# Two heads' scores in 64 array rows each, unpadded keys, one copy for q and k, one score buffer of two banks, scores behind the products of a step

## The reference

```
n = layer_norm(x);  x = x + attention(n, n)            # self:  20 heads of 64, 128 queries, 128 keys
n = layer_norm(x);  x = x + attention(n, context)      # cross: 20 heads of 64, 128 queries, 77 keys
x = geglu_ff(layer_norm(x)) + x
# layer 1: 20 heads of width 8, 73 text keys and 4 image keys, softmax, mask, output product, residual
attention: sim = (q @ k.T) * 64**-0.5; p = softmax(sim); out = p @ v; out @ wo + bo
```

## Time and profile before

| what | value |
|---|---|
| median of 3 runs | 3806.16 us (3804.15 to 3810.74) |
| span of the profiled execution | 3799.1 us |
| TensorE matmul busy | 3608.9 us, 95% |
| TensorE weight loads busy | 3328.8 us, 88% |
| VectorE, ScalarE, GpSimd busy | 2547.7, 2592.4, 1352.4 us |
| mean granted TensorE clock | 0.995 |

### The profile page before, as it was taken

The page is one execution under the profiler, slowest core; times in us unless marked ns, Lnnn a source line. Parts: engine busy times, 40 slices in busy tenths (PEclk is TensorE's granted clock), DMA queues, the critical chain, the costliest instruction groups (busy, mean ns, idle before and its releaser), DMA issues.

```text
span 3799.1 us, 88944 instructions
## 1 busy us (share of the span) xinstructions
PE 3608.9 (95%) x29708; PEld 3328.8 (88%) x29708; DVE 2547.7 (67%) x8159; ACT 2592.4 (68%) x8021; POOL 1352.4 (36%) x1658
## 2 busy tenths in 40 slices
PE   6999999999999999999999999999999999999997
PEld 5888989889898898988989899898988989889897
DVE  6667666676766666676676766767667676666766
ACT  6667676766767667676676766767676676766764
POOL 2233343333433334333333433334333343333433
PEclk9999999999999999999999999999999999999998
DMA  6522314223142321413223132231422313232130
GB/s 169 163 64 75 103 44 119 60 85 91 41 122 58 96 77 51 123 47 106 70 60 117 45 112 65 76 103 44 121 57 87 90 41 121 58 96 77 53 93 18
DMA packets 210716, 313.38 MB, mean 82 GB/s; under 512 B 31232, under 2 KB 167520, under 8 KB 210272
## 3 DMA queue, kind: packets, MB, share of 16 engines
q1 hardware_dynamic: 209984, 307.53, 27.6%
q10 hardware_dynamic: 288, 0.16, 0.0%
HBM read 267.97 MB, written 14.42 MB: 74 GB/s over the span
## 4 chain that ended last, share of the span: by engine, by line
PE 60%; DVE 17%; ACT 11%; issue 8%; POOL 4%; DMA 1%; SPq 0%; ACTq 0%; DVEq 0%; POOLq 0%
PE PS L818 8%; PE PT L840 6%; PE PV L854 6%; PE PW L798 5%; PE PG L659 5%; ACT SE L989 4%; PE PG L651 4%; PE PG L634 4%; PE PV L864 3%; DVE sums L1233 3%; PE PG L637 3%; PE PG L635 3%; PE PG L636 3%; POOL SE L1404 3%; PE PG L742 2%
## 5 line engine op out<-in xcount | busy, mean ns | idle before, releaser
L1404 POOL TENSOR_TENSOR SE<-SE,rs 128x512 f32<-128x512 f32 (+1 forms) x640 | 557.6, 871 | 1761.8 <-DVE rs L1238 1761.8
L989 ACT ACTIVATE SE<-PS,mx 128x128 f32<-128x128 f32 (+2 forms) x3840 | 982.6, 346 | 240.7 <-DVE qq L1262 128.5
L975 ACT ACTIVATE PTs<-PT 128x512 f32<-128x512 f32 (+2 forms) x960 | 575.4, 599 | 87.1 <-PE PT L840 67.9
L840 PE MATMUL PT<-ident,SE 128*128 128x128 f32 (+2 forms) x3840 | 582.0, 274 | 36.4 <-POOL SE L1404 34.6
L1233 DVE TENSOR_REDUCE sums<-SE 128x4 f32<-128x512 f32 (+1 forms) x640 | 367.0, 573 | 337.8 <-ACT SE L989 336.9
L1222 DVE TENSOR_REDUCE mx<-PS 128x4 f32<-128x512 f32 (+2 forms) x960 | 504.4, 525 | 72.1 <-PE PS L818 58.7
L840 PEld LDWEIGHTS PT<-ident,SE 128*128 128x128 f32 (+2 forms) x3840 | 465.5, 144 | 64.5 <-POOL SE L1404 49.0
L1396 POOL TENSOR_TENSOR n<-qq,p_half 128x4 f32<-128x4 f32 x320 | 345.3, 1079 | 490.2 <-DVE qq L1262 490.1
L798 PE MATMUL PW<-w_o,OTs 128*128 128x160 f32 x2560 | 415.3, 299 | 1.1 <-ACT OTs L967 1.1
L818 PE MATMUL PS<-qk 128*128 128x256 f32 x1280 | 348.5, 395 | 47.6 <-ACT qk L915 47.6
L912 ACT ACTIVATE qk<-PG 128x256 f32<-128x256 f32 x640 | 252.9, 395 | 190.1 <-PE PG L637 186.5
(11 more groups left out here) (207 smaller groups left out, 7828.5 us busy)
## 6 DMA issues: line engine op xcount, KB each, us to landing
q_slice<-q_split SPq DMA_DIRECT2D x630, 192.0 KB, 2.4
vc_slice<-vc_split SPq DMA_DIRECT2D x155, 512.0 KB, 3.6
kc_slice<-kc_split SPq DMA_DIRECT2D x150, 256.0 KB, 2.7
q1st<-q_hi SPq DMA_DIRECT2D x320, 32.0 KB, 1.9
k1st<-k_hi SPq DMA_DIRECT2D x160, 38.5 KB, 1.9
xres<-in_x_dram SPq DMA_DIRECT2D x32, 160.0 KB, 2.3
q1st<-q_lo SPq DMA_DIRECT2D x160, 32.0 KB, 1.9
out_dram<-x SPq DMA_DIRECT2D x64, 80.0 KB, 1.6
```

Of the source, the lines that this page charges most:

```text
L840: last = tr(PT[0:J, 128 * i:128 * i + 128], SE[:, place % 4, J * i:J * i + J], ident[:, :])
L975: a_(PTs[0:J, place % 3, :], PT[0:J, :], ACT.Copy).then_inc(S["pts_done"], 1)
L989: last = a_(SE[:, place % 4, J * i:J * i + J], PS[place % 2][:, step * i:step * i + J], ACT.Exp, bias=mx[:, place % 2, i:i + 1])
L1404: gp.tensor_tensor(e, e, rs[:, n % 2, :].unsqueeze(2).to_broadcast([128, 4, J]), ALU.mult)\
```

## The change

- q is scaled by SCALE0 when its weights are split (SPLIT_SCALE, `slice_high`, `slice_low`), not when it is copied out.
- Job "qk" is read out by one copy of 512 (self) or 256 columns (cross) in place of three or one; "kc" by one copy on each of ScalarE and VectorE in place of two. Keys are no longer padded, and the memsets for the padding go.
- The scores of a head take 64 rows of the array: four matmuls of 128 or 77 columns for a unit, alternately on rows 0 to 63 (into bank 0 of PS) and rows 64 to 127 (into bank 1).
- PS is one buffer of two banks: `scores` waits for the exponentials of the unit just before.
- On TensorE `scores` moves from the start of a step behind `probs_v`; `probs_transposed` moves behind "v" and `wo`. The lists of the other engines keep their order.

```diff
-        PS = [ctx.enter_context(nc.psum_tensor(f"PS{i}", [128, 512], fp32)) for i in range(2)]
+        PS = ctx.enter_context(nc.psum_tensor("PS", [128, 2, 512], fp32))
...
                 def scores(u):
                     place, (layer, g, n) = PLACE[u], u
-                    if place >= 2:
-                        pe.wait_ge(S["exp_done"], place - 1)
-                        layer0, g0, n0 = UNITS[place - 2]
-                        if layer0 == "l1":
-                            pe.wait_ge(S["sip_in"], l1_count(g0, n0))
-                    ps = PS[place % 2]
+                    if place >= 1:
+                        pe.wait_ge(S["exp_done"], place)
...
-                        keys = qk[:, n % 2, 1:3, :]
+                        keys = qk[:, n % 2, 1, :]
...
                         for b in range(HB):
-                            last = mm(ps[:, 2 * J * b:2 * J * b + 2 * J], qk[:, n % 2, 0, 128 * b:128 * b + 128],
-                                      keys[:, :, J * b:J * b + J], start=True, stop=True)
+                            for e in range(2):
+                                rows = slice(DH * e, DH * e + DH)
+                                last = mm(PS[:, e, J * b:J * b + J],
+                                          qk[rows, n % 2, 0, 128 * b:128 * b + 128],
+                                          keys[rows, J * b:J * b + J], start=True, stop=True)
...
                 for t in range(FIRST, LAST):
                     if t == KEEP_BUSY:
                         keep_busy(20)
-                    if t + 1 in UNIT_AT:
-                        scores(UNIT_AT[t + 1])
                     for name in qk_at(t):
                         job(name)
-                    if t - PT_LAG in UNIT_AT:
-                        probs_transposed(UNIT_AT[t - PT_LAG])
                     for name in late_at(t):
                         if name[0] == "v":
                             job(name)
                     for u in outputs_at(t):
                         if u[0] == "l0":
                             wo(*u[1:])
+                    if t - PT_LAG in UNIT_AT:
+                        probs_transposed(UNIT_AT[t - PT_LAG])
                     for u in products_at(t):
                         probs_v(u)
+                    if t + 1 in UNIT_AT:
+                        scores(UNIT_AT[t + 1])
...
                     elif kind == "qk":
                         ps = take(name)
-                        last = a_(qk[:, i % 2, 0, :], ps[:, 0:HT], ACT.Copy, scale=SCALE0)
-                        if i < U0:
-                            for e in range(2):
-                                last = a_(qk[DH * e:DH * e + DH, i % 2, 1 + e, :], ps[DH * e:DH * e + DH, HT:2 * HT],
-                                          ACT.Copy)
-                        last.then_inc(S["qk_done"], 1)
+                        w = 2 if i < U0 else 1
+                        a_(qk[:, i % 2, 0:w, :].rearrange("p a n -> p (a n)"), ps[:, 0:w * HT], ACT.Copy)\
+                            .then_inc(S["qk_done"], 1)
```

More of the change, by code:

```diff
@@ L267, in _ @@
                 nc.vector.memset(gv[:, :, :, :], 1.0)
-                nc.vector.memset(qk[:, :, :, :], 0.0)
             @block.gpsimd
@@ L984, in exp @@
                             act.wait_ge(S["qq_done"], l1_count(g0, n0))
-                    J, step = (K0[n // U0],) * 2 if layer == "l0" else (TT, T)
+                    J = K0[n // U0] if layer == "l0" else TT
                     if layer == "l1":
@@ L988, in exp @@
                     for i in range(4):
-                        last = a_(SE[:, place % 4, J * i:J * i + J], PS[place % 2][:, step * i:step * i + J], ACT.Exp,
-                                  bias=mx[:, place % 2, i:i + 1])
+                        scored = PS[:, i // 2, J * (i % 2):J * (i % 2) + J] if layer == "l0" else PS[:, 0, T * i:T * i + J]
+                        last = a_(SE[:, place % 4, J * i:J * i + J], scored, ACT.Exp, bias=mx[:, place % 2, i:i + 1])
                     last.then_inc(S["exp_done"], 1)
@@ L1148, in job @@
                         if (g, i) == (0, 0):
-                            dve.wait_ge(keys_zero, 1)
+                            dve.wait_ge(S["split_done"], 6)
                         dve.wait_ge(S["kc_done"], NP * g + i + 1)
-                        for e in range(2):
-                            rows = slice(DH * e, DH * e + DH)
-                            last = v.tensor_copy(kx[1][rows, i, e, :].rearrange("p (b t) -> p b t", t=T),
-                                                 ps[rows, HB * TS:2 * HB * TS].rearrange("p (b t) -> p b t", t=TS)[:, :, 0:T])
-                        last.then_inc(S["kc_dve"], 1)
+                        v.tensor_copy(kx[1][:, i, 0, :].rearrange("p (b t) -> p b t", t=T),
+                                      ps[:, HB * TS:2 * HB * TS].rearrange("p (b t) -> p b t", t=TS)[:, :, 0:T])\
+                            .then_inc(S["kc_dve"], 1)
                     elif kind == "v":
@@ L1219, in softmax_in @@
                     dve.wait_ge(S["s_done"], place + 1)
-                    J, step = (K0[n // U0],) * 2 if layer == "l0" else (TT, T)
-                    sc = PS[place % 2][:, 0:4 * step].rearrange("p (i j) -> p i j", j=step)
-                    v.tensor_reduce(mx[:, place % 2, :], sc[:, :, 0:J], AX, ALU.max, negate=True).then_inc(S["mx_done"], 1)
-                    if layer == "l1":
+                    if layer == "l0":
+                        J = K0[n // U0]
+                        sc = PS[:, :, 0:2 * J].rearrange("p e (b j) -> p e b j", j=J)
+                        v.tensor_reduce(mx[:, place % 2, :].rearrange("p (e b) -> p e b", b=2), sc, AX, ALU.max, negate=True)\
+                            .then_inc(S["mx_done"], 1)
+                    else:
+                        sc = PS[:, 0, 0:4 * T].rearrange("p (i j) -> p i j", j=T)
+                        v.tensor_reduce(mx[:, place % 2, :], sc[:, :, 0:TT], AX, ALU.max, negate=True).then_inc(S["mx_done"], 1)
                         b, w = n // W1, n % W1
@@ L1292, in split_low @@
                             rows = slice(M * r, M * r + M)
-                            last = v.tensor_tensor(hi[rows], raw[rows], hi[rows].bitcast(fp32), ALU.subtract)
+                            last = v.scalar_tensor_tensor(hi[rows], raw[rows], scale, hi[rows].bitcast(fp32),
+                                                          ALU.mult, ALU.subtract)
                         last.then_inc(S["split_done"], 1)
```

42 lines of the change are left out of this document (20 added, 22 removed).

## The result

| | before | after |
|---|---|---|
| median | 3808.45 us (4 runs, 3804.15 to 3812.24) | 4536.1 us (4 runs, 4529.21 to 4540.7) |
| ratio | | 1.191, 95% interval 1.1895 to 1.1928 |
| profiled span | 3799.1 us | 4538.9 us |
| TensorE busy | 3608.9 us, 95% | 3907.6 us, 86% |
| TensorE idle (span less busy) | 190 us | 631 us |

The change made the kernel 19% slower, 436 us more than the 4100 us forecast, and beyond the upper end of the range (4420). Of the 740 us of span, 441 are TensorE's idle time (269 in the forecast) and 299 its busy time (28 in the forecast).

A forecast was written before the change was run, and what follows sets the result against it. TensorE, 95% busy, was the bound. 3799.1 + 28 - 48 + 267 + 17 + 23 + 70 - 60 = 4096 us of span, plus 7 to the median, said as 4100; forecast 4020 to 4180, range 3900 to 4420.

The forecast's parts named there:

- The pauses for banks that VectorE frees: TensorE jobs wait for bank reads queued behind the late scores' maxima: 20 jobs a group, 16.7 us a group, +267 us.
- The 17 us for ScalarE's copy of q: Three jobs a group wait for ScalarE's copy of q, which stands behind the exponentials: 0.35 us each, +17 us.
- the 60 us taken as covered: Part of the new TensorE waits falls on pauses that exist already: -60 us, between 0 and 142.
- The single chain behind `unit_out`: TensorE stands still from the scores' end through maxima, `unit_out` and the "kc" read: 2.2 us a pause.
- faster with free banks: Rival: VectorE's bank reads end before TensorE asks, no new wait comes, 3786 us; chance 0.06.
- 0.44 + 0.09 + 0.09 = 0.62: Split score group on TensorE: 0.44 us for four pairs of matmuls, 0.09 for each drain entering and leaving the tile size.
- Tiles in turn: Rival: the split score matmuls run one behind the other, a pair costs 0.22 us, 4380 us in all; chance 0.18.
- The halved scores: Rival: changing tile size costs nothing, no pause comes, each score group's busy time halves, 3467 us; chance 0.03.
- +28 us of occupancy: Score matmuls split by rows on TensorE: self units -39 us, cross units +67 us, together +28 us.
- the loop of the single buffer: Scores wait for exponentials to free the one buffer: 1.93 us between self groups, four short steps a group, +23 us.
- the later probabilities, +70 us: Probabilities reach PT 4.0 us after the scores end; nine places a group are short, 0.48 us each, +70 us.
- the 48 that went: TensorE's wait for ScalarE's copy of q and k ahead of the scores, 47.6 us, goes: -48 us.

The follow-up runs named there:

- e7_reads_first: The changed kernel with VectorE reading the kc and v banks ahead of the maxima of the next unit: 4298 us, ratio 1.129.
- e2_pos_one: The kernel before with the scores in the late place, also waiting for the exponentials of the unit just before, as with one buffer: 4618 us, ratio 1.213.
- e5_rows: The changed kernel with the qk and kc copies of the kernel before, scores still split by rows: 4572 us, ratio 1.201.
- e6_filled: The changed kernel with unused identity matmuls behind the scores of four units in groups 1 to 14: 4463 us, ratio 1.172.
- e3_se5: The changed kernel with five SE buffers for the exponentials' results in place of four: 4412 us, ratio 1.160.
- e1_pos: The kernel before with only TensorE's order changed: scores behind `probs_v`, PT behind v and `wo`, both score buffers kept: 4504 us, ratio 1.183.
- e4_a_first: The changed kernel with TensorE's order of before, scores at the start of the step, one score buffer kept: 5505 us, ratio 1.447.

## Why the prediction was wrong, and where it was right

In one paragraph: the chain that the forecast built on was right in kind and size, and the sum over it was too short by 436 us. It counted a pause as its idle time and nothing else, with the clock left where it was, and it left out three waits (for an SE buffer, for a table load, and of `wo`). The place of the scores was put at 246 us and cost 699.

**Right: the direction, and the term it rested on.** The pauses for banks that VectorE frees were put at 267 us. The rows rose from 77 to 335, by 258. That is so near that some luck is in it, since not every wait came as long as counted (three of the five pauses of about 2 us). The 17 us for ScalarE's copy of q did not come (4.4 us). Nor is there a sign of the 60 us taken as covered: rows that stood before stand unchanged, such as PT's 34.6 and 34.1 us. The single chain behind `unit_out` was 2.13 us for 2.2, and e7_reads_first removed it as the mechanism demands. The rival "faster with free banks" is out: its limit was 20 us of new pauses.

**Right: how split tiles run.** A self group of the changed kernel (L776 is another job's transposition):

```profile
1184.04 0.71 PE L813 MATMUL PS<-qk 64*128 64x128 f32 x8
1184.69 0.33 PE L776 MATMUL PG<-ident,o 128*128 128x128 f32 x1
```

From L813's first start to the next instruction it takes 0.65 us, and 0.60 for cross (1538.14 to 1538.74, where L631 started). The forecast's terms for that stretch were 0.44 + 0.09 + 0.09 = 0.62. The trace's single records start two at a time, 7 ns apart: at 1184.04, 1184.26, 1184.37 and 1184.48 us. "Tiles in turn" would have needed 0.44 more, 1.09 us. The Trainium skill, "TensorE: Matmul & The Clock Gate", Part 3, The mechanism, says that a weight load overlaps matmuls in flight only when its row group differs. Exposed loads within a row group would cost about what "tiles in turn" does, and the trace doesn't bear that out. The halved scores didn't come either. But the sign of the term was wrong for this kernel: the forecast had +28 us of occupancy, and the split took 46 us off (e2_pos_one to e5_rows); idle time fell by 45. That its value was in how soon the scores end is argued.

**Wrong: the clock was not in the sum.** This is the largest omission, about 157 us. Before, the mean clock was 0.995 and pauses near 2 us were few; the forecast added such pauses, five in each group (three came at that length), and left the clock where it was. In the changed kernel 58 of 78 falls lie behind units 7, 20, 22, 50 and 53 of a group, and ahead of most of them TensorE had stood still in one pause of 1.2 to 2.1 us; the pause of 2.1 us behind unit 13 brought none. The Trainium skill, "TensorE: Matmul & The Clock Gate", HAM oscillation — how this bites in real kernels, describes a kernel that falls to the low clock again and again behind waits, and counts half of the time spent there as lost. The runs come near it: e6_filled gives 0.41 us for each us.

**Wrong: the loop of the single buffer, 23 us.** The step "0.03 + 0.67 + 0.04 + 1.13 + 0.06 = 1.93 us" took each chain with nothing in it but maxima and exponentials. `exp` also waits for `qq_done` of the l1 unit four places back, which stands among the waits of before and which the prediction doesn't mention:

```profile
ACT SE L989 <- DVE qq L1262: 128.5, 138, 2.0
```

The loop measured 166 us of waits, of which e3_se5 removed 111. There is another guest: where exponentials follow the feed-forward's activation, ScalarE loads a table first, hidden before and now inside the loop:

```profile
1682.24 1.28 ACT L982 ACT_TABLE_LOAD   x1
...
1683.54 0.96 ACT L982 ACTIVATE SE<-PS,mx 128x73 f32<-128x73 f32 x4
...
1684.55 0.42 PE L822 MATMUL PS<-kbd,q1st 96*128 96x308 f32 x1 [1.54 <-ACT SE L982]
```

There are 32 such loads in either kernel. In the changed one the next scores waited behind every one of them, 32 us in all, and in the kernel before behind none. The same 32 us are in the 55 us that e3_se5 leaves, so some 23 us remain, the size of the forecast's term: what was wrong is what it left out of the loop. (In time one buffer cost 114 us, e1_pos to e2_pos_one.)

**Wrong: `wo` had no term.** It moved ahead of PT and lost the scores ahead of it, which had covered ScalarE's copy of the outputs; before it waited 1.1 us in all, now 47.3, and 92.4 in e1_pos.

**Wrong: the later probabilities, +70 us.** PT's wait for GpSimd is 34.1 us where it was 34.6. A likely reason is that the chain of 4.0 us fits into steps that the other pauses had made longer (4536 / 960 = 4.7 us a step). In e1_pos, where nothing waits for the exponentials, it shows (54.2 us). The terms of the sum were each counted against the old length of a step, as if they were independent.

**The sum again**, in us of span: idle +441 (job banks +258, exponentials 166 less the 48 that went, `wo` +46, the rest small), clock about +157, and some 140 that remain in the busy time. A part of these belongs to the pauses too. An instruction of 256 columns is busy for 0.28 us while the next would start 0.11 to 0.12 behind it, so each wait costs some 0.16 more than its idle time shows, and there are 495 more waits: about 80 us. And the instruction behind a wait takes longer until the next starts, here 0.22 us in place of 0.12:

```profile
1679.55 0.39 PE L631 MATMUL PG<-nT,w_hi 128*128 128x256 f32 x1 [0.21 <-DVE later L1155]
...
1679.77 0.28 PE L632 MATMUL PG<-nT,w_lo 128*128 128x256 f32 x1
...
1679.89 0.28 PE L633 MATMUL PG<-nT,w_hi 128*128 128x256 f32 x1
```

Over all lines but the split scores that is 52 us at full clock, and 22 before, so 30 more. The 80 us are argued from the rows, not tested, and with them some 30 us stay open; a clock that cost its upper bound of 184 us would close them. e1_pos has nearly the same remainder with the old matmuls, so it is not the split by rows.

By parts of the edit, measured: the place +699 (forecast 246: 267 + 17 + 70 - 48 - 60), one buffer +114 (23), split by rows -46 (+28), copies -36 (0). The parts are measured in this order, each on top of the one before, and another order gives other sizes: with one buffer, the split and the copies in place, the late scores save 969 us (e4_a_first).

## What to carry to other kernels

In a kernel bound by one engine, work that others wait for belongs at the head of its step, as long as what it waits for itself is ready there (with one score buffer it was not, and the head was the dearer place). What a later place costs is read from what is queued behind the waiting instruction on the next engine. New pauses have to be priced with the time at the low clock and the slower ends and starts around them; here TensorE's busy time grew by two thirds as much as its idle time (299 us for 441). When a buffer is taken away, every wait of the producer goes into the loop, also one for a third engine; look for it in the wait list of the engine that frees the buffer. A read must stand in its engine's list where its producer stands in the other: the same edit gained 5% with late scores and lost 3% with early ones.

## What the hardware showed beyond that

- Two row halves of 64 x 128 with float32 operands run side by side: eight instructions of 128 columns start two at a time and end 0.71 us after the first start, and the group costs 0.20 us from the instruction before it and 0.65 us to the next.
- Most of the 78 stretches at 1.2 GHz came behind a pause of TensorE of 1.2 to 2.1 us and lasted 3 to 7 us, and they cost 0.41 us of time for each us. Pauses of 2.1 us at one place of 15 groups brought none. Fourteen instructions without use (1.83 us) in a pause kept the clock at 2.4 GHz at another, and the kernel with more work was 73 us faster.
- An instruction of 256 columns behind a wait took 0.22 us until the next one's start, and 0.12 us without a wait.
- A table load on ScalarE between two kinds of activation took 1.28 us, and the exponentials started 0.02 us behind its end.
